# A linear attention layer on one core: values and gates as seven half products over two pairs of heads

## The chip, the cores and the metric

The kernel runs on 1 core of a Trainium2 chip. The metric is the time of one execution in device microseconds (us), of which the median of some runs is taken. TensorE (PE) multiplies matrices, VectorE (DVE), ScalarE (ACT) and GpSimd (POOL) work elementwise, SyncE (SP) issues transfers. DRAM is the device's memory; SBUF and PSUM are on the core, and PE writes only PSUM.

## What is computed

The program is two blocks of a network over 2048 tokens of 512 features: a recurrent unit, a state space layer, feed forward layers, an attention, two mixtures of experts. The change touches one layer, the linear attention (`L1_attn_b`), which takes the normalized residual x:

```
qkv = silu(x @ qkv_w.T)                    # 32 heads of 64, each with q, k, v
per head and block i of tokens:
    intra = ((q_i @ k_i.T) * decay) @ v_i
    inter = (q_i * query_decay) @ state
    state = state * block_decay + (k_i * key_decay).T @ v_i
attn = rmsnorm(intra + inter over all heads) * norm_w
y    = (sigmoid(x @ gate_w.T) * attn) @ out_w.T
```

## The kernel before

Every layer is a stage of its own: it has a program for each engine, and all engines meet at its end. The linear attention consists of three stages. `lina` (`normalized_features`, L131) normalizes the residual `g.X` and transposes it to `lin_z`, features by tokens. `linb` (`linear_heads`, L2241) is the part that the change is about. `linc` is the output projection.

`linb` works through 16 pairs of heads n. Each pair is 128 features wide and has four quarters q of 512 tokens, each of four chunks of 128. For a quarter PE does `keys_first` (the scores `s_ps`, and `tr_ps`, the transposed keys), `additions` (`kv_ps`, what the keys and values add to the state) and `outputs` (`o_ps`, from the values and from the state). DVE multiplies queries by decays (`qd`) and scores by decays (`aw`), updates the state (`update`) and makes the `gated` result, which SP stores. ACT copies `tr_ps` with a decay (`kt`) and `o_ps` to `osb`. POOL squares `osb` (`linb_sq`) and adds it up in `lin_squares`.

Among this, PE computes the next pair's features, in three banks of PSUM, `pr_ps`. `piece` (L2409) makes the values in the first quarter (kind 2: tokens as the stationary operand, matmuls of 128 columns) and the gates in the second (kind 3: weights as the stationary operand, 512 columns), over all of the 512 features, and ACT takes each out of its bank through silu or sigmoid. In the third and fourth quarters `seven` (L2437) makes queries and keys together, for half of the tokens each: a product of 2 x 2 blocks (two weight blocks by two halves of the features, against two halves of the features by two quarters of the tokens) as seven products of half the depth in place of eight. These need sums of the weights, which POOL makes (`weight_sums`, L2378, four a pair), sums of the tokens' features, which DVE makes once (`token_sums`, L2630, eight, stored where the residual was), and then, on the way out, a copy `p1` on ACT and five sums u2, u3, kB, kA, qB on DVE, with silu on ACT behind them. PE issues the products in the order p1, p6, p2, p7, p5, p4, p3; p7 waits for u2, p4 for u3, p3 for kB. The first two stand ahead of `additions`, the others behind it. Queries, keys and gates lie in `proj`, values in `vt`, both for two pairs in turn.

The order on each engine is that of the code, and semaphores hold the engines together. The stage begins with POOL's constants (decay tables, 64 small memsets for the slopes); PE waits for all of them (L2521), and ACT then computes the decays, 32 single columns of `kdec` among them. SP loads pair 0's weights, copies the residual to DRAM (`normalized_rows`, since the token sums overwrite it), and clears `residual_rows`, 4 MB, with `linb_nothing` once the constants are there. It fetches the residual back at the last pair.

## Time and profile before

| | us |
|---|---|
| median of 3 runs | 5027.12 (5025.49 to 5028.86) |
| the profiled execution | 5025.78 |
| its span | 5024.1 |
| stage `linb` in it, from the first instruction to the last square | 2934.6 to 4095.6 |
| PE busy in the span | 4532.5 |

All times of the trace are microseconds from the span's start. A line number is the code line before the change; a matmul with f32 operands stands in the trace as two instructions.

### The profile page before, as it was taken

The numbers are of one execution on the slowest core, as the hardware profiler recorded it, in microseconds if no ns is written. First come the engines' busy times: TensorE is split into PE (matmuls) and PEld (weight loads), VectorE is DVE, ScalarE is ACT, GpSimd is POOL, SyncE is SP. The second block draws the span as 40 slices with busy tenths as digits, with TensorE's granted clock in tenths as the row PEclk, the third lists the DMA queues.
The fourth block names the chain that finished last, engine by engine and source line by source line (L and its number), as shares of the span: only waits on it lengthen the run. The fifth ranks groups of instructions, "written<-read, shape, count | busy, mean of one in ns | idle before, by whom it ended". The sixth has DMA issues, their size and how long they took to land. (4 is left out here: it accounts for less than half of the span.)

```text
span 5024.1 us, 65280 instructions
## 1 busy us (share of the span) xinstructions
PE 4532.5 (90%) x26052; PEld 2544.3 (51%) x26052; DVE 2503.2 (50%) x3810; ACT 1646.6 (33%) x2825; POOL 1704.5 (34%) x1130
## 2 busy tenths in 40 slices
PE   6359997899999999978999859999999989699996
PEld 3124443433333333245666536666666658566663
DVE  7865888367777777852222234444443444512222
ACT  5414443211555556822111123323333210321110
POOL 2000000101888887024555411222222210155553
PEclk9679998999999999988999979999999999799998
DMA  2000000100000000036888740000010033378897
GB/s 75 0 16 7 7 0 31 40 1 1 2 1 2 1 1 1 1 129 182 257 257 258 168 157 24 32 32 32 25 33 32 24 132 105 134 223 257 257 257 198
DMA packets 241716, 425.99 MB, mean 85 GB/s; under 512 B 31504, under 2 KB 119568, under 8 KB 241424
## 3 DMA queue, kind: packets, MB, share of 16 engines
q1 hardware_dynamic: 184080, 279.28, 16.7%
q0 software_dynamic: 57344, 142.64, 11.6%
q8 instruction: 205, 3.36, 0.3%
q14 instruction: 87, 0.71, 0.0%
HBM read 301.73 MB, written 120.13 MB: 84 GB/s over the span
## 5 line engine op out<-in xcount | busy, mean ns | idle before, releaser
L1557 ACT ACTIVATE attc_prob<-attc_ps 128x512 f32<-128x512 f32 x1024 | 547.6, 597 | 299.0 <-PE attc_ps L1473 289.8
L1589 DVE TENSOR_REDUCE attc_peak<-attc_ps 128x1 f32<-128x512 f32 x768 | 490.7, 682 | 204.6 <-PE attc_ps L1481 204.6
L1444 POOL TENSOR_TENSOR attc_acc<-attc_acc,attc_prob 128x2048 f32<-128x2048 f32 x120 | 543.3, 4528 | 40.4 <-ACT attc_prob L1557 26.5
L1481 PE MATMUL attc_ps<-att_k,att_q 32*128 32x512 f32 x1536 | 492.0, 641 | 0.0
L1473 PE MATMUL attc_ps<-att_q,att_k 32*128 32x512 f32 x2048 | 459.7, 589 | 0.0
L2398 POOL TENSOR_TENSOR linb_sq<-linb_osb 128x512 f32<-128x512 f32 x64 | 90.8, 1419 | 847.3 <-ACT linb_osb L2588 847.3
L1493 PE MATMUL attc_ps<-attc_prob,att_v 128*32 128x256 f32 (+1 forms) x3472 | 310.4, 429 | 0.4 <-ACT attc_prob L1557 0.4
L1074 DVE TENSOR_TENSOR_SCAN ssmb_state<-ssmb_decay,ssmb_bu 128x2048 f32<-128x2048 f32 x64 | 280.7, 4413 | 54.2 <-PE ssmb_y_ps L927 29.4
L2072 POOL DMA_INDIRECT residual_rows<-moe2c_ye,moe2w_index x128 | 201.7, 1575 | 230.1 <-DVE moe2c_ye L2195 200.2
L2072 POOL DMA_INDIRECT residual_rows<-moe1c_ye,moe1w_index x128 | 201.5, 1575 | 230.0 <-DVE moe1c_ye L2195 200.0
L2698 DVE SCALAR_TENSOR_TENSOR linb_gated<-linb_osb,linb_norm_w,linb_proj 128x512 f32<-128x512 f32 x64 | 61.3, 957 | 400.4 <-ACT linb_osb L2588 400.4
L927 PE MATMUL ssmb_y_ps<-ssmb_state,ssmb_diag 128*128 128x512 f32 x512 | 234.9, 606 | 19.5 <-DVE ssmb_y L1083 9.9
L2424 PE MATMUL linb_pr_ps<-linb_wt,lin_z 128*128 128x128 f32 x2048 | 236.3, 277 | 17.0 <-POOL linb_slope_own L2375 17.0
L783 POOL MEMSET ffn_nothing<- 128x512 f32 x2 | 1.0, 524 | 716.6 <-POOLq L61 716.6
L2424 PEld LDWEIGHTS linb_pr_ps<-linb_wt,lin_z 128*128 128x128 f32 x2048 | 233.5, 194 | 17.2 <-POOL linb_slope_own L2375 17.2
L1493 PEld LDWEIGHTS attc_ps<-attc_prob,att_v 128*32 128x32 f32 x3472 | 68.4, 108 | 329.5 <-ACT attc_prob L1557 180.2
L2105 PE MATMUL moe2c_gu_ps<-moe2c_xt,moe2w_wgu 128*128 128x256 f32 x1024 | 232.5, 381 | 0.0
L2105 PE MATMUL moe1c_gu_ps<-moe1c_xt,moe1w_wgu 128*128 128x256 f32 x1024 | 232.4, 380 | 0.0
L2428 PE MATMUL linb_pr_ps<-lin_z,linb_wt 128*128 128x512 f32 x512 | 224.9, 592 | 0.0
L2187 DVE TENSOR_TENSOR moe1c_h<-moe1c_sg,moe1c_gu_ps 128x256 f32<-128x256 f32 x96 | 40.4, 421 | 326.3 <-ACT moe1c_sg L2169 309.3
L2187 DVE TENSOR_TENSOR moe2c_h<-moe2c_sg,moe2c_gu_ps 128x256 f32<-128x256 f32 x96 | 40.4, 421 | 326.2 <-ACT moe2c_sg L2169 309.3
L2105 PEld LDWEIGHTS moe2c_gu_ps<-moe2c_xt,moe2w_wgu 128*128 128x128 f32 x1024 | 190.6, 191 | 23.5
(488 smaller groups left out, 8545.8 us busy)
## 6 DMA issues: line engine op xcount, KB each, us to landing
moe1w_wgu<-in_L_ffn_gate_up_proj SPq DMA_DIRECT2D x32, 1536.0 KB
moe2w_wgu<-in_L_ffn_gate_up_proj SPq DMA_DIRECT2D x32, 1536.0 KB
moe1w_wd<-in_L_ffn_down_proj SPq DMA_DIRECT2D x32, 512.0 KB
gated_features<-linb_gated SPq DMA_DIRECT2D x64, 256.0 KB, 2.3
moe2w_wd<-in_L_ffn_down_proj SPq DMA_DIRECT2D x32, 512.0 KB
linc_gt<-gated_features SPq DMA_DIRECT2D x7, 2048.0 KB, 8.6
linb_wt<-in_L_attn_b_qkv_w SPq DMA_DIRECT2D x16, 768.0 KB, 4.8
residual_rows<-residual SPq DMA_DIRECT2D x8, 1024.0 KB, 4.3
```

The lines of the kernel that those rows point to most:

```text
L927: last = nc.tensor.matmul(y_ps[:, t, :], diag[:, s % DIAGS, :], state[:, s % RING, t * NB:(t + 1) * NB], start=(n == 0), stop=(n == N_STAT ...
L1074: V.tensor_tensor_scan(state[:, s % RING, :], decay[:, s % RING, :], bu[:, e % 2, :], 0.0, ALU.mult, ALU.add).then_inc(state_done, 1)
L1444: pool.tensor_tensor(to, before, prob[:, U % NP, :, :], ALU.add).then_inc(pool_done, 2 if at % HALF == 1 else 1)
L1473: nc.tensor.matmul(ps[:, bank_of(("score", U, h)), :], k[own, f, keys], q[own, f, cols], start=False, stop=True).then_inc(s_done, 1)
L1481: nc.tensor.matmul(ps[:, take("peak", U, h), :], q[own, f, i * P:(i + 1) * P], k[own, f, b * NB:(b + 1) * NB], start=True, stop=True).then ...
L1493: last = nc.tensor.matmul(o_bank[h * DH:(h + 1) * DH, cols], v[:, i, at:at + DH], prob[:, U % NP, h, cols], start=(i == 0), stop=(i == TT ...
L1557: nc.scalar.activation(prob[:, U % NP, h, :], ps[:, bank_of(("score", U, h)), :], ACT.Exp).then_inc(exp_done, 1)
L1589: V.tensor_reduce(peak[:, w // TT % 2, i % QH, h, b:b + 1], ps[:, bank_of(("peak", U, h)), :], axis=AX.X, op=ALU.max).then_inc(mx_used, 1)
L2072: pool.indirect_dma_start(out=g.y_dram[x], out_offset=bass.IndirectOffsetOnAxis(ap=index[:, n // 2, n % 2:n % 2 + 1], axis=0), in_=ye[:, y ...
L2105: last = nc.tensor.matmul(gu_ps[:, x, part, :], wgu[:, j % PW, x, k, part * IN:part * IN + P], xt[:, j % 2, x, k, :], start=(k == 0), stop ...
L2424: last = nc.tensor.matmul(bank[:, c * CH:(c + 1) * CH], z[:, k, (t * TQ + c) * CH:(t * TQ + c + 1) * CH], wt[:, b, kind, k, :], start=(k = ...
L2428: last = nc.tensor.matmul(bank, wt[:, b, kind, k, :], z[:, k, tokens(t)], start=(k == 0), stop=(k == DT - 1))
```

## The change

Values and gates are now also made by `seven`, over two pairs of heads m at once (the two weight blocks are then the two pairs) and half of the tokens. So each pair n computes ahead one seven of values, one of gates and two of queries and keys: in an even pair values and gates of the late half of the tokens for this pair and the next, in an odd pair those of the early half for the next two. A table `sevens` sets the order. Values and gates keep early and late halves in buffers of their own; queries and keys lie in one buffer, `qk`, for one pair, and ACT waits for `qd` before it writes there. Each kind has its own weight sums (`wsum` is three times as large), POOL makes those of values and gates once in two pairs, and the weights of values and gates lie in a buffer `wvg` outside the stage. Its first contents and the copy of the residual to DRAM are loaded and stored in the norm stage (`moves`). At the start, four sevens come without a wait for the constants; POOL makes three groups of weight sums ahead of the constants; the decays come between two results of the third seven, with `kdec` in one instruction. (The code that `seven_out` and `sums` share with before is the same but for the place of the result.)

```diff
-def normalized_features(nc, g, name, zt, weights=()):
...
-            if weights:
-                sp.wait_ge(w_loaded, 16 * len(weights))
+            for to, source in moves:
+                sp.dma_start(to, source).then_inc(w_loaded, 16)
+            if weights or moves:
+                sp.wait_ge(w_loaded, 16 * (len(weights) + len(moves)))
...
+def value_weights(g, m):
+    return g.dram["L1_attn_b_qkv_w"][2 * m:2 * m + 2, :, 2, :, :].rearrange("n p k f -> p n k f")
+
+
+def gate_weights(g, m):
+    return g.dram["L1_attn_b_gate_w"][2 * m:2 * m + 2, :, :, :].rearrange("n p k f -> p n k f")
...
+        with nc.sbuf_tensor("lin_z", [P, DT, T], F32) as z, nc.sbuf_tensor("lin_wvg", [P, 2, 2, DT, P], F32) as wvg:
+            x_rows = g.z_dram[0:T, 0:D].rearrange("(i p) d -> p i d", p=P)
+            normalized_features(nc, g, "lina", z, moves=((wvg[:, 0, :, :, :], value_weights(g, 0)), (wvg[:, 1, :, :, :], gate_weights(g, 0)),
+                                                         (x_rows, g.X[:, :, :])))
+            linear_heads(nc, g, "linb", z, wvg, x_rows, squares)
...
-        wt = L.sb("wt", [P, 2, KINDS, DT, P])
-        proj = [L.sb(f"proj{b}", [P, 3, T]) for b in range(2)]
...
+        first = [(VALUES, 0, 0), (GATES, 0, 0), (QK, 0, 0), (QK, 0, 1)]
+
+        def sevens_of(n):
+            if n + 1 == PAIRS_L:
+                return []
+            early = [(VALUES, n // 2, 1), (GATES, n // 2, 1)] if n % 2 == 0 else [(VALUES, n // 2 + 1, 0), (GATES, n // 2 + 1, 0)]
+            return early + [(QK, n + 1, 0), (QK, n + 1, 1)]
+
+        sevens = first + [s for n in range(PAIRS_L) for s in sevens_of(n)]
+        place = {what: i for i, what in enumerate(sevens)}
+        wqk = L.sb("wqk", [P, 2, 2, DT, P])
+        qk = L.sb("qk", [P, 2, T])
+        g_early, g_late = L.sb("g_early", [P, 3, 2, NB]), L.sb("g_late", [P, 2, 2, NB])
+        v_early, v_late = L.sb("v_early", [P, 3, HC, P]), L.sb("v_late", [P, 2, HC, P])
...
+        def needed_by(n, q):
+            return (QK, n, q // 2) if q < 2 or n % 2 or n + 1 == PAIRS_L else (GATES, n // 2, 1)
...
+        def weights(kind, m):
+            return wqk[:, m % 2, :, :, :] if kind == QK else wvg[:, kind, :, :, :]
+
+        def values(n, c):
+            return v_early[:, n % 3, c, :] if c < HC else v_late[:, n % 2, c - HC, :]
+
+        def gates(n, q):
+            return g_early[:, n % 3, q, :] if q < 2 else g_late[:, n % 2, q - 2, :]
+
+        def result(kind, m, half, t):
+            if kind == QK:
+                return qk[:, half, tokens(t)]
+            if kind == GATES:
+                return gates(2 * m + half, t)
+            rows = v_early[:, (2 * m + half) % 3, :, :] if t < 2 else v_late[:, half, :, :]
+            return rows[:, t % 2 * TQ:(t % 2 + 1) * TQ, :].rearrange("p c f -> p (c f)")
...
+            def load(n):
+                sp.dma_start(wqk[:, n % 2, :, :, :], qkv_rows[n, :, 0:2, :, :]).then_inc(w_loaded[n % 2], 16)
+
+            load(0)
+            load(1)
...
             for n in range(PAIRS_L):
                 if n + 2 < PAIRS_L:
-                    reload(n, n % 2)
+                    sp.wait_ge(pr_done, after_seven((QK, n, 1)))
+                    load(n + 2)
...
+                    sp.wait_ge(gated_done, n * TC + (q + 1))
+                    sp.dma_start(out_rows[:, n, tokens(q)], gated[:, q % 2, :]).then_inc(saved[q % 2], 16)
+                    if n % 2 == 0 and n + 2 < PAIRS_L and q == 0:
+                        sp.wait_ge(pr_done, after_seven((VALUES, n // 2, 1)))
+                        sp.dma_start(wvg[:, VALUES, :, :, :], value_weights(g, n // 2 + 1)).then_inc(v_loaded, 16)
+                    if n % 2 == 0 and n + 2 < PAIRS_L and q == 1:
+                        sp.wait_ge(pr_done, after_seven((GATES, n // 2, 1)))
+                        sp.dma_start(wvg[:, GATES, :, :, :], gate_weights(g, n // 2 + 1)).then_inc(g_loaded, 16)
...
+                if kind == QK:
+                    pool.wait_ge(w_loaded[m % 2], 16 * (m // 2 + 1))
+                elif m:
+                    pool.wait_ge(v_loaded if kind == VALUES else g_loaded, 16 * m)
+                if m:
+                    pool.wait_ge(pr_done, after_seven((kind, m - 1, 1)))
...
+            weight_sums(VALUES, 0)
+            weight_sums(GATES, 0)
+            weight_sums(QK, 0)
...
-            link(pool.memset(state[:, :, :], 0.0))
-            link(pool.memset(squares[:, :], 0.0))
-            link(pool.memset(nothing[:, :], 0.0))
             for h, s in enumerate(head_slopes()):
                 link(pool.memset(slope_all[:, h:h + 1], -s))
                 r = (h % 2) * LD
                 link(pool.memset(slope_own[r:r + LD, h // 2:h // 2 + 1], -s))
+            link(pool.tensor_tensor(until[:, :], until[:, :], slope_all[:, :], ALU.mult))
+            link(pool.memset(state[:, :, :], 0.0))
+            link(pool.memset(squares[:, :], 0.0))
+            link(pool.memset(nothing[:, :], 0.0))
             assert link.n == N_CONSTS
...
+            for n in range(PAIRS_L):
+                if n + 1 < PAIRS_L:
+                    weight_sums(QK, n + 1)
                 for q in range(TC):
+                    if q == 2 and n % 2 == 0 and n + 2 < PAIRS_L:
+                        weight_sums(VALUES, n // 2 + 1)
+                        weight_sums(GATES, n // 2 + 1)
                     m = n * TC + q
-                    pool.wait_ge(o_out, m + 3)
+                    pool.wait_ge(o_out, m + 1)
                     pool.tensor_tensor(sq[:, :], osb[:, q % 2, :], osb[:, q % 2, :], ALU.mult).then_inc(sq_step, 1)
...
+            def product(kind, bank, w, x, fresh):
+                for c in range(TQ if kind == VALUES else 1):
+                    chunk = slice(c * CH, (c + 1) * CH)
+                    for k in range(HK):
+                        if kind == VALUES:
+                            last = nc.tensor.matmul(pr_ps[:, bank, chunk], x[:, k, chunk], w[:, k, :],
+                                                    start=(fresh and c == 0 and k == 0), stop=(k == HK - 1), skip_group_check=True)
+                        else:
+                            last = nc.tensor.matmul(pr_ps[:, bank, :], w[:, k, :], x[:, k, :],
+                                                    start=(fresh and k == 0), stop=(k == HK - 1), skip_group_check=not fresh)
                 last.then_inc(pr_done, 1)
...
                 if "p1" in some:
-                    pe.wait_ge(pr_out, n * FROM_BANKS + (2 * TC + 2 if x else 2 * TC - 1))
-                    product(one, a11, b11, True)
+                    if kind == QK:
+                        pe.wait_ge(w_loaded[m % 2], 16 * (m // 2 + 1))
+                    elif m:
+                        pe.wait_ge(v_loaded if kind == VALUES else g_loaded, 16 * m)
+                    if i:
+                        pe.wait_ge(pr_out, 2 * i)
+                    product(kind, one, a11, b11, True)
                 if "p6" in some:
...
+                if q % 2 == 0:
+                    pe.wait_ge(pr_out, copies_of(needed_by(n, q)))
+                    pe.wait_ge(finished, finished_of(needed_by(n, q)))
+                if m:
+                    pe.wait_ge(aw_done, m)
...
-            pe.sem_inc(kv_done, 1)
-            pe.wait_ge(consts, N_CONSTS)
-            for kind in (2, 3):
-                for t in range(TC):
-                    piece(kind, t, 0, 0, 0)
-            for x in range(2):
-                seven(0, 0, x, PRODUCTS)
...
+            for what in first:
+                seven(what, PRODUCTS)
+            for n in range(PAIRS_L):
+                more = sevens_of(n)
                 for q in range(TC):
-                    keys_first(n, b, q)
-                    if more and q < 2:
-                        piece(q + 2, 0, n + 1, r + b, 1 - b)
-                    elif more:
-                        seven(n + 1, 1 - b, q - 2, PRODUCTS[0:2])
-                    additions(n, b, q)
-                    if more and q < 2:
-                        for t in range(1, TC):
-                            piece(q + 2, t, n + 1, r + b, 1 - b)
-                    elif more:
-                        seven(n + 1, 1 - b, q - 2, PRODUCTS[2:])
-                    outputs(n, b, q)
-
-            over_pairs(body)
+                    keys_first(n, q)
+                    if more:
+                        seven(more[q], PRODUCTS[0:2])
+                    additions(n, q)
+                    if more:
+                        seven(more[q], PRODUCTS[2:])
+                    outputs(n, q)
...
+            def decays():
+                act.wait_ge(consts, N_CONSTS)
+                nc.scalar.activation(sdec[:, :], slope_own[:, :], ACT.Exp, scale=float(CH)).then_inc(tables0, 1)
+                nc.scalar.activation(kdec[:, :], until[:, :], ACT.Exp).then_inc(tables0, 1)
+                table(0)
...
+                nc.scalar.activation(result(kind, m, 0, 2 * x), pr_ps[:, 0, :], shape).then_inc(pr_out, 1)
+                if what == (QK, 0, 0):
+                    decays()
+                for name, half, t in (("kB", 1, 2 * x + 1), ("kA", 1, 2 * x), ("qB", 0, 2 * x + 1)):
+                    act.wait_ge(added, after_sum(i, name))
+                    to = result(kind, m, half, t)
+                    nc.scalar.activation(to, to, shape).then_inc(finished, 1)
...
-                        for t in range(TC):
-                            piece_out(q + 2, t, n + 1, 1 - b)
+                        act.wait_ge(qd_done, n * TC + q + 1)
+                        seven_out(more[q])
                         if q == 1:
-                            table(n + 1, 1 - b)
-                    elif more:
-                        seven_out(n + 1, 1 - b, q - 2)
+                            table(n + 1)
                     quarter_out(n, q)
...
+            for x in range(2):
+                token_sums(x)
+            for what in first:
+                sums(what, SUMS)
+            dve.wait_ge(tables0, 2)
+            dve.wait_ge(norm_loaded, 16)
+            for n in range(PAIRS_L):
+                more = sevens_of(n)
                 dve.wait_ge(tables, n * 3 + 3)
...
+                    if q % 2 == 0:
+                        dve.wait_ge(pr_out, copies_of(needed_by(n, q)))
+                        dve.wait_ge(finished, finished_of(needed_by(n, q)))
+                    if m:
+                        dve.wait_ge(o_done, m)
+                    V.tensor_tensor(qd[:, :].rearrange("p (c i) -> p c i", i=CH), qk[:, 0, tokens(q)].rearrange("p (c i) -> p c i", i=CH),
...
-                    if more and q >= 2:
-                        sums(n + 1, 1 - b, q - 2, ("u2",))
+                                    dd[:, n % 2, :, :].rearrange("p h (o i) -> p h o i", o=1).to_broadcast([P, 2, TQ, CH]), ALU.mult).then_inc(aw_done, 1)
+                    if more:
+                        sums(more[q], ("u2",))
                     update(n, q)
...
+                    if more:
+                        sums(more[q], SUMS[1:])
+                    dve.wait_ge(o_out, m + 1)
+                    if m >= 2:
...
-            dve.wait_ge(x_spilled, 16)
-            for x in range(2):
-                token_sums(x)
-            for x in range(2):
-                sums(0, 0, x, SUMS)
-            over_pairs(body)
```

How this stands on the engines. The counts here are those of the program, half of the trace's for matmuls. PE, from the start of `linb` (the names are output<-operands), before:

```order
L2424 MATMUL linb_pr_ps<-linb_wt,lin_z 128x128 x64
L2428 MATMUL linb_pr_ps<-lin_z,linb_wt 128x512 x16
L2433 MATMUL linb_pr_ps<-lin_z,linb_wt 128x512 x2
L2433 MATMUL linb_pr_ps<-residual,linb_wsum 128x512 x2
L2433 MATMUL linb_pr_ps<-lin_z,linb_wt 128x512 x2
```

and with the change (one whole seven of values, then the one of gates begins):

```order
L2459 MATMUL linb_pr_ps<-lin_wvg,lin_z 128x128 x8
L2459 MATMUL linb_pr_ps<-linb_wsum,residual 128x128 x8
L2459 MATMUL linb_pr_ps<-lin_wvg,lin_z 128x128 x8
L2459 MATMUL linb_pr_ps<-linb_wsum,residual 128x128 x16
L2459 MATMUL linb_pr_ps<-lin_wvg,residual 128x128 x8
L2459 MATMUL linb_pr_ps<-linb_wsum,lin_z 128x128 x8
L2462 MATMUL linb_pr_ps<-lin_z,lin_wvg 128x512 x2
```

64 small matmuls of values are now 56, and those of gates, 16, are 14. The second product and those behind it have sums as operands.

PE, first quarter of the first pair, from the scores to the outputs, before:

```order
L2482 MATMUL linb_s_ps<-linb_proj 128x128 x8
L2488 MATMUL linb_tr_ps<-ident,linb_proj 128x128 x4
L2424 MATMUL linb_pr_ps<-linb_wt,lin_z 128x128 x16
L2497 MATMUL linb_kv_ps<-linb_vt,linb_kt 128x128 x4
L2424 MATMUL linb_pr_ps<-linb_wt,lin_z 128x128 x48
L2509 MATMUL linb_o_ps<-linb_aw,linb_vt 64x128 x8
```

and with the change:

```order
L2517 MATMUL linb_s_ps<-linb_qk 128x128 x8
L2524 MATMUL linb_tr_ps<-ident,linb_qk 128x128 x4
L2459 MATMUL linb_pr_ps<-lin_wvg,lin_z 128x128 x8
L2459 MATMUL linb_pr_ps<-linb_wsum,residual 128x128 x8
L2533 MATMUL linb_kv_ps<-linb_v_early,linb_kt 128x128 x4
L2459 MATMUL linb_pr_ps<-lin_wvg,lin_z 128x128 x8
L2459 MATMUL linb_pr_ps<-linb_wsum,residual 128x128 x16
L2459 MATMUL linb_pr_ps<-lin_wvg,residual 128x128 x8
L2459 MATMUL linb_pr_ps<-linb_wsum,lin_z 128x128 x8
L2545 MATMUL linb_o_ps<-linb_aw,linb_v_early 64x128 x8
```

The four pieces of values became seven products, two of them ahead of `linb_kv_ps` as in the other quarters.

SP, from the start of the norm stage `lina` (whose first row is the first branch), before:

```order
L140 UNCONDITIONAL_BRANCH
L2313 UNCONDITIONAL_BRANCH
L2316 DMA linb_wt<-in_L_attn_b_qkv_w 128x1536
L2317 DMA linb_wt<-in_L_attn_b_gate_w 128x512
L2335 DMA normalized_rows<-residual 128x16x512
```

and with the change:

```order
L140 UNCONDITIONAL_BRANCH
L145 DMA lin_wvg<-in_L_attn_b_qkv_w 128x2x512
L145 DMA lin_wvg<-in_L_attn_b_gate_w 128x2x512
L145 DMA normalized_rows<-residual 128x16x512
L58 UNCONDITIONAL_BRANCH
L2359 UNCONDITIONAL_BRANCH
L2362 DMA linb_wqk<-in_L_attn_b_qkv_w 128x1024 x2
```

The residual's copy and 1 MB of weights moved from `linb` into `lina`, and the weights of queries and keys alone stayed.

## Rows read from the trace of the kernel before

**Rows 1.** Page, part 1: busy us, share of the span, instructions.

```profile
PE 4532.5 (90%) x26052; PEld 2544.3 (51%) x26052; DVE 2503.2 (50%) x3810; ACT 1646.6 (33%) x2825; POOL 1704.5 (34%) x1130
```

**Rows 2.** Busy time by stretches: start:end, length, engines, clock, DMA share, GB/s.

```profile
core 0: us, PE busy (x) PEld busy (x) DVE busy (x) ACT busy (x) POOL busy (x), PEclk, DMA share, GB/s
3080.00:4010.00 930.00, 930.00 (x5604) 622.21 (x5603) 380.61 (x685) 279.72 (x472) 197.41 (x161) 1.00 0.09 30
```

**Rows 3.** In order of time, PE, POOL, DVE: start, length, engine, line, what, [idle before].

```profile
3570.79 3.74 PE L2424 MATMUL linb_pr_ps<-linb_wt,lin_z 128*128 128x128 f32 x32
...
3574.36 1.06 PE L2497 MATMUL linb_kv_ps<-linb_vt,linb_kt 128*128 128x128 f32 x8
...
3571.65 1.60 POOL L2400 TENSOR_TENSOR lin_squares<-lin_squares,linb_sq 128x512 f32<-128x512 f32 x1
...
3572.05 1.21 DVE L2689 TENSOR_TENSOR linb_aw<-linb_s_ps,linb_dd 128x1024 f32<-128x1024 f32 x1
```

**Rows 4.** In order of time, PE, start and end of the layer.

```profile
2950.11 16.95 PE L2424 MATMUL linb_pr_ps<-linb_wt,lin_z 128*128 128x128 f32 x128 [16.97 <-POOL linb_slope_own L2375]
...
2980.63 1.88 PE L2433 MATMUL linb_pr_ps<-lin_z,linb_wt 128*128 128x512 f32 x4
...
2992.65 1.88 PE L2433 MATMUL linb_pr_ps<-lin_z,linb_wt 128*128 128x512 f32 x4
...
3006.32 1.16 PE L2482 MATMUL linb_s_ps<-linb_proj 64*128 64x128 f32 x16 [1.49 <-issue]
...
4061.72 1.16 PE L2482 MATMUL linb_s_ps<-linb_proj 64*128 64x128 f32 x16
```

**Rows 5.** In order of time, POOL and DVE, the sums at the start.

```profile
2950.24 0.73 POOL L2385 TENSOR_TENSOR linb_wsum<-linb_wt 128x256 f32<-128x256 f32 x1 [0.19 <-POOL linb_slope_own L2375]
...
2956.27 1.23 DVE L2634 TENSOR_TENSOR residual<-lin_z 128x1024 f32<-128x1024 f32 x1 [23.91 <-ACT linb_kdec L2595]
...
2964.46 1.23 DVE L2639 TENSOR_TENSOR residual<-lin_z,residual 128x1024 f32<-128x1024 f32 x1
```

**Rows 6.** In order of time, ACT, POOL, DVE, from second to third quarter.

```profile
3604.37 0.60 ACT L2560 ACTIVATE linb_proj<-linb_pr_ps 128x512 f32<-128x512 f32 x1 [2.84 <-PE linb_pr_ps L2428]
...
3607.88 1.54 POOL L2398 TENSOR_TENSOR linb_sq<-linb_osb 128x512 f32<-128x512 f32 x1 [16.44 <-ACT linb_osb L2588]
3609.50 1.60 POOL L2400 TENSOR_TENSOR lin_squares<-lin_squares,linb_sq 128x512 f32<-128x512 f32 x1
...
3608.67 1.30 DVE L2686 TENSOR_TENSOR linb_qd<-linb_proj,linb_qdec 128x512 f32<-128x512 f32 x1
...
3611.60 0.69 DVE L2647 TENSOR_TENSOR linb_u<-linb_pr_ps,linb_p 128x512 f32<-128x512 f32 x1 [0.37 <-PE linb_pr_ps L2433]
```

**Rows 7.** In order of time, PE and ACT, end of a seven.

```profile
3619.16 1.88 PE L2433 MATMUL linb_pr_ps<-lin_z,linb_wsum 128*128 128x512 f32 x4
...
3623.08 1.16 PE L2482 MATMUL linb_s_ps<-linb_proj 64*128 64x128 f32 x16
...
3621.80 0.63 ACT L2571 ACTIVATE linb_proj<-linb_proj 128x512 f32<-128x512 f32 x1 [1.09 <-DVE linb_proj L2657]
```

**Rows 8.** In order of time, SyncE and ACT; transfers: count, KB each, us to landing.

```profile
2934.58 0.35 SPq L2316 DMA_DIRECT2D linb_wt<-in_L_attn_b_qkv_w  x1
...
2935.45 0.43 SPq L2335 DMA_DIRECT2D normalized_rows<-residual  x1
...
2916.77 1.28 ACT L128 ACT_TABLE_LOAD   x1 [56.00 <-PEq L61]
...
2932.81 1.07 ACT L184 COPY lin_z<-lina_zt_ps 128x512 f32 x2 [0.54 <-PE lina_zt_ps L169]
...
normalized_rows<-residual SPq DMA_DIRECT2D x1, 4096.0 KB, 15.6
```

**Rows 9.** Busy time by stretches: first products, last pair.

```profile
2950.00:2952.00 2.00, 1.89 (x9) 1.89 (x10) 0.00 (x0) 1.91 (x11) 1.81 (x4) 0.50 1.02 414
...
4074.00:4076.00 2.00, 0.66 (x11) 0.45 (x8) 1.48 (x6) 0.00 (x0) 0.00 (x0) 1.00 1.05 389
```

326 lines of the change are left out of this document (121 added, 205 removed).

## The prediction

> **What bounds the kernel now.** I read the page's line on TensorE (PE) first, then the stretches of the layer, then one pair in order of time, then the layer's first 75 us engine by engine, then the transfers. Over the whole program PE is busy 90% of the time [rows 1]. Inside this layer, from 3080 to 4010 us, it is busy 930.00 of 930.00 us at a granted clock of 1.00, while DVE, ACT and POOL are busy 41%, 30% and 21% of it [rows 2]. So here only PE's own work counts, and time taken off it is gained as long as no other engine becomes late. From the first scores at 3006.32 to those of the last pair at 4061.72 [rows 4] it is 1055.40 us, 15 periods of 70.36 us, one for each pair that computes the next one's features ahead. The one place where PE waits long is the start: the first product comes at 2950.11, after 16.97 us of idleness that POOL's constants end [rows 4].
>
> **The loop (removed PE work).** A values matmul of 128 columns costs 0.1116 us of PE: 32 of them from 3570.79 to 3574.36 [rows 3]. One of 512 columns costs 0.4293 us: the 28 of one seven take 2980.63 to 2992.65, 12.02 us [rows 4]. (The trace shows each matmul of the program twice.) Before, a pair costs 128 of the first and 32 of the second for values and gates: 14.28 + 13.74 = 28.02 us. After, it costs one values seven, 7 products of 16 small ones, 112 x 0.1116 = 12.50 us, and one gates seven, 28 x 0.4293 = 12.02 us: 24.52 us. The gain is 3.50 us per pair, for 15 pairs: **-52.5 us**, a period of 66.86 us. Both kinds are issued back to back in the trace before, so I take no other price for them.
>
> **The loop (added work).** Each of these sevens adds five sums on DVE at 0.69 us and one more pass of 0.6 us on ACT, about 7 us of DVE per pair; with 41% busy it has room. What counts is whether PE waits in the middle. The nearest rows are the sevens of queries and keys, which already run with no wait of PE, beside the largest batch of state updates. Three differences remain.
> (1) After the gates seven, the last result goes through DVE and ACT, which in a seven ends 1.55 us behind PE's last product (3619.16 + 1.72 = 3620.88, ACT done at 3621.80 + 0.63) [rows 7]; before, ACT's pass over the last gates product began 0.2 us behind it, at 3604.37, and took 0.60, 0.8 in all [rows 6]. So tables, output copy, gated result and aw come 0.75 us later in the next quarter. There u2 would start at 3611.60 + 0.75 and end at 3613.04, and the product behind it starts at 3614.00 (3619.16 less three products of 1.72) [rows 6, 7]: 1.0 us to spare. Cost 0.
> (2) In even pairs the scores of the third quarter now wait for that gates seven. They start 2.20 us behind its last product, as the scores at 3623.08 do behind 3620.88 [rows 7], and its result is there after 1.55: 0.65 us to spare. In return no pair's first scores wait for the seven just ahead. Cost 0.
> (3) ACT now waits for qd ahead of each seven; behind that wait stand the copy of p1 and the finishing passes, and for the copy wait u2 and PE's third product. In the third quarter qd ends at 3608.67 + 1.30 = 3609.97, with (1) at 3610.72, and the copy ends at 3611.3; PE's third product starts at 3612.28. Cost 0.
> From the other side: should all three bite, I bound them by 1 us a pair, 15 us.
>
> **POOL and DVE.** POOL gets eight more weight sums per two pairs, 0.73 us each [rows 5], 5.8 us, in the third quarter of even pairs, behind the square and the sum that end at 3609.50 + 1.60 = 3611.10 [rows 6]; the next square comes a quarter, some 16 us, later. Do they hold up DVE? In the trace they collide where both operands lie in SBUF: qd takes 1.30 us and u2, of the same size but out of PSUM, 0.69 [rows 6]. POOL's square ends at 3607.88 + 1.54 = 3609.42, and qd, started at 3608.67, ends 0.55 behind that; they take turns. The new sums fall beside DVE's sums out of PSUM, and such an instruction isn't held: aw, 1024 columns out of PSUM, takes 1.21 us wholly beside POOL's sum of 3571.65 to 3573.25 [rows 3], as long as a token sum of 1024 columns alone, 1.22 [rows 5]. Cost 0.
> The Trainium skill ("SBUF — State Buffer", "Who interferes with whom") states the same as a rule: a DVE instruction with two SBUF inputs and a GpSimd instruction that reads SBUF exclude each other for the whole instruction, with at most one SBUF input DVE is free. By its letter every token sum at the start would wait for one weight sum, 8 x 1.90 = 15.2 us, and the start would gain 11.7 us.
>
> **The start.** PE no longer waits for the constants. The stage's first instructions stand at 2934.6 [rows 8]. p1 of values runs at once. p6 needs four token sums (DVE) and four weight sums (POOL), and p7 needs u2, which stands behind all eight token sums. These last 9.42 us alone (2956.27 to 2964.46 + 1.23), 1.17 each [rows 5]; if they take turns with POOL's at 0.73, 1.90 each, 15.2 us. I take 14.0, nearer to turns, because of the qd row. u2 ends at 2934.6 + 14.0 + 0.8 = 2949.4. Then four products of values, 7.14, and three sevens, 36.06: 2992.6. Before, the first 128 matmuls took from 2950.11 to 2966.89 (2980.63 less 32 of 0.4293), 16.8 us rather than 14.3 [rows 4], since the clock first stood at 0.50 [rows 9]; now p6 and p2 run in that time, so I add 0.8 (bounds 0 and 2.5): 2993.4. The first scores follow at once, for they wait only for the first half of queries and keys. Before they stand at 3006.32 [rows 4]: **-12.9 us**. Bounds: -18.3 (no turns, no cold clock) and -10.0 (full turns, full loss). ACT needs the constants only in the third seven, near 2974; POOL, with twelve sums (to 2951.5) and 15.6 us of constants (2934.6 to 2950.2) [rows 5, 8], has them at 2967: 7 us to spare. The 4 MB of clearing transfers start there too and, at the 15.6 us that 4 MB take [rows 8], end before the loop's first load at 2993.
>
> **The norm stage (moved transfers).** The 4 MB copy of the residual and 1 MB of weights now start with the norm stage, at 2916.77 [rows 8] less some 0.1, and its end waits for them. Before, the first issue was at 2934.58, and the copy, issued at 2935.45 behind the same 1 MB, landed 15.6 us later, at 2951.05: 16.5 us in all [rows 8]. That gives 2933.2, and ACT's last copy there ends at 2933.88 [rows 8]. **Hidden, by 0.7 us**; cost 0. If the new weight loads, in runs of 2 KB, went at half rate, 2.6 us more, and the start would be 2 us later.
>
> The tail (last pair, the way back of the residual) is the same work behind the same product. **Sum**: -52.5 - 12.9 = -65.4 us against the profiled execution's 5025.8 (its span of 5024.1 and 1.7 around it), 4960.4; the median of 5027.1 lies 1.3 above that, so 4961.7 us.
>
> **Rivals.**
> A. *As above*, 4961.7, each term within its bounds. For it: PE without any wait in 930 us, and sevens already in that run.
> B. *New waits inside the loop.* The margins of 0.65 and 1.0 us are eaten (DVE behind POOL in the third quarter, the finishing pass late); 30 new sevens at 0.5 us cost 15: 4976.7.
> C. *No turns at the start.* Token sums at 1.17 us each: u2 at 2944.8, scores at 2988.8, -17.5 instead of -12.9: 4957.1. Against it: the qd row.
> D. *The residual's copy ends the norm stage.* It lands 4 us later than reckoned: 4965.7. For it: only 0.7 us to spare.
> E. *The change doesn't give what it says*: a small matmul in a seven would not keep 0.1116 us but cost 0.128 (14.28 over 112); the values seven is then as dear as the plain one, +1.8 x 16: 4990. Against it: in size and kind the instructions are the same.
> F. *Slower than before: the clock.* If PE's waits in the new sevens got long enough to pull the granted clock to 0.50 (the 1.2 GHz level), each us of work costs two. It decides once 65.4 us of the loop's work, 4.4 us of each pair's 66.9, run at that level beyond what waits cost; with a quarter of each pair so, 16.7 us x 15 = 250 us: 5212. Against it: in the last pair PE is busy 0.66 of 2.00 us in a stretch and its clock stays at 1.00 [rows 9]; it fell only over the 17 us of full idleness ahead of 2950.
>
> **How the numbers follow.** A 0.68, B 0.13, C 0.09, D 0.04, E 0.03, F 0.03. The time is that of A. The range goes from 4953 (C, less what median and profile differ by and 3 us) to 4976 (D whole, B nearly): it leaves out F, E and the end of B, and the unforeseen. A measurement of this kernel can tell about 0.2%, 10 us, from no change; A to E are all faster by more: faster 0.96, same 0.01, slower 0.03.
>
> **What would show it.** In the profile of the changed kernel: a period of 66.9 us from pair to pair, PE busy throughout at clock 1.00; the first scores about 58.8 us after the layer's first instruction (71.7 before); token sums with 1.7 to 1.9 us between starts; ACT's first exponentials without a wait for POOL; the norm stage no longer than 18 us. Wrong it would be with a PE wait ahead of p7, p4 or the third quarter's scores, or a norm stage that ends with a wait of SyncE.

## The result, and the profile after

The changed kernel takes 4963.79 us (median of 4 runs, 4961.65 to 4964.71) beside 5027.61 us for the kernel before on the same chip: a ratio of 0.9873, with a 95% interval of 0.9857 to 0.9888. It is 63.8 us faster. The forecast was 4961.7 us, a gain of 65.4.

The page's first part of the changed kernel, which answers to [rows 1], and then its busy time in the loop (start:end, length, then the engines, the granted clock, the share of the DMA engines, GB/s), which answers to [rows 2]:

```profile
PE 4478.5 (90%) x25730; PEld 2509.3 (51%) x25732; DVE 2621.7 (53%) x3970; ACT 1663.2 (34%) x2827; POOL 1754.6 (35%) x1195
```

```profile
3080.00:3940.00 860.00, 860.00 (x5117) 566.61 (x5116) 465.08 (x802) 290.48 (x488) 222.78 (x203) 1.00 0.10 31
```

PE still has no idle time at all in the loop, at a clock of 1.00. DVE went from 41% to 54% of it (465.08 of 860.00), and that costs nothing.

PE in order of time in the changed kernel, as in [rows 4] (start, length, engine, line, what, [idle before, what ended it]): the first products of the layer, its first scores, and those of the last pair.

```profile
2935.79 3.48 PE L2459 MATMUL linb_pr_ps<-lin_wvg,lin_z 128*128 128x128 f32 x16 [1.45 <-PEq L61]
2942.76 3.61 PE L2459 MATMUL linb_pr_ps<-linb_wsum,residual 128*128 128x128 f32 x16 [3.50 <-DVE residual L2645]
2946.17 2.03 PE L2459 MATMUL linb_pr_ps<-lin_wvg,lin_z 128*128 128x128 f32 x16
2949.98 3.84 PE L2459 MATMUL linb_pr_ps<-linb_wsum,residual 128*128 128x128 f32 x32 [1.78 <-DVE linb_u L2655]
...
2957.23 1.88 PE L2462 MATMUL linb_pr_ps<-lin_z,lin_wvg 128*128 128x512 f32 x4
...
2993.38 1.16 PE L2517 MATMUL linb_s_ps<-linb_qk 64*128 64x128 f32 x16
...
3996.27 1.16 PE L2517 MATMUL linb_s_ps<-linb_qk 64*128 64x128 f32 x16
```

From the first scores to those of the last pair it is 1002.89 us, 15 periods of 66.86 (before 1055.40, 70.36). The stage `linb` starts with SyncE's load at 2935.75, so the first scores stand 57.6 us into it (before 71.7). The 16.97 us for which PE waited for POOL's constants are gone. What is left are 3.50 us until four token sums are there (the second product, p6) and 1.78 until u2 is (the fourth, p7).

The norm stage, SyncE and ACT in order of time, and the issue's row (KB, us to landing), as in [rows 8]:

```profile
2918.76 0.46 SPq L145 DMA_DIRECT2D normalized_rows<-residual  x1
...
2935.75 0.82 SPq L2362 DMA_DIRECT2D linb_wqk<-in_L_attn_b_qkv_w  x2
...
2917.83 1.28 ACT L128 ACT_TABLE_LOAD   x1 [55.68 <-PEq L61]
...
2933.91 1.13 ACT L186 COPY lin_z<-lina_zt_ps 128x512 f32 x2 [0.48 <-PE lina_zt_ps L171]
```

```profile
normalized_rows<-residual SPq DMA_DIRECT2D x1, 4096.0 KB, 15.5
```

The copy lands at 2918.76 + 15.5 = 2934.3, ACT ends at 2933.91 + 1.13 = 2935.04: the copy is hidden, and the stage takes 17.9 us (2917.83 to 2935.75) where it took 17.8.

**Where the 63.8 us are.** The loop gives 52.5 and the start 14.1, together 66.6. The last pair and the way to the next stage `linc` take 35.25 us (3996.27 to 4031.52) where they took 35.47. The profiled executions differ by 64.3 us in their spans, so 2.3 are lost elsewhere, in code that the change doesn't touch: 1.1 ahead of the norm stage and 1.8 where the last layer goes from routing to experts (over six microseconds at the experts' first large products the granted clock was 0.80 before, 4400 to 4406 us, and 0.59 now, 4334 to 4340), and 0.6 won in between. Over the fourteen profiles of this study the norm stage starts anywhere from 2916.77 to 2920.67, with the same code ahead of it. That spread is as large as some effects below, so these are read inside the stage: **scores** is the distance from the start of `linb` (SyncE's first load) to its first scores, **tail** from the last pair's first scores to PE's first matmul of `linc`.

| kernel | median us | norm stage | scores | period | tail |
|---|---|---|---|---|---|
| before | 5027.6 to 5028.3 | 17.8 | 71.7 | 70.36 | 35.5 |
| changed | 4963.8 | 17.9 | 57.6 | 66.86 | 35.3 |
| changed, again | 4964.4 | 17.7 | 57.6 | 66.86 | 37.9 |
| eighth | 5019.0 | 17.9 | 61.1 | 70.36 | 35.3 |
| spill_back | 4975.5 | 17.8 | 68.7 | 66.86 | 36.7 |
| consts_first | 4971.9 | 17.9 | 70.1 | 66.86 | 35.3 |
| pool_yields | 4960.1 | 18.1 | 55.6 | 66.86 | 36.2 |
| norm_5mb | 4962.5 | 19.6 | 57.6 | 66.86 | 35.3 |
| pad2 | 4964.0 | 17.8 | 57.6 | 66.86 | 35.3 |
| pad4 | 4991.0 | 18.0 | 57.6 | 67.9, then 68.93 | 35.3 |
| pad6 | 5083.8 | 17.7 | 57.6 | 71.4, then 73.8 to 75.6 | 36.4 |
| pool_double | 4963.9 | 18.0 | 57.6 | 66.86 | 35.3 |
| late_token_sums | 4960.2 | 17.8 | 55.5 | 66.86 | 35.3 |
| early_p2 | 4959.3 | 17.7 | 53.2 | 66.86 | 36.4 |

Medians are of 4 runs (eighth 10, pool_double one; before 4 to 13). The last four columns are from one profiled execution of each kernel. Where a median and these columns differ by some microseconds (consts_first is 8.2 above the changed kernel in the median and 11.8 in the profiled execution), the difference is no larger than the spread just named.

### The profile page after: what moved, and what is told of

It reads as the page before. It is cut to its first block and busy times, and to the rows that moved or that the text cites. A ratio compares the mean times of both kernels' runs of the same rounds, so it can differ in the third digit from the quotient of the medians.

```text
span 4959.8 us, 64998 instructions
## 1 busy us (share of the span) xinstructions
PE 4478.5 (90%) x25730; PEld 2509.3 (51%) x25732; DVE 2621.7 (53%) x3970; ACT 1663.2 (34%) x2827; POOL 1754.6 (35%) x1195
## 3 DMA queue, kind: packets, MB, share of 16 engines
q0 software_dynamic: 57344, 142.64, 11.8%
## 5 line engine op out<-in xcount | busy, mean ns | idle before, releaser
L2462 PE MATMUL linb_pr_ps<-residual,linb_wsum 128*128 128x512 f32 x576 | 262.9, 593 | 0.0
L2107 PEld LDWEIGHTS moe1c_gu_ps<-moe1c_xt,moe1w_wgu 128*128 128x128 f32 x1024 | 190.9, 191 | 23.0
L1306 DVE TENSOR_REDUCE attb_peak<-attb_mx_ps 128x2 f32<-128x1024 f32 x128 | 150.9, 1221 | 94.1 <-PE attb_mx_ps L1245 93.9
L2462 PEld LDWEIGHTS linb_pr_ps<-residual,linb_wsum 128*128 128x128 f32 x576 | 109.7, 190 | 137.5 <-issue 137.5
```

The lines of the kernel that those rows point to most:

```text
L1306: V.tensor_reduce(peak[:, tb % 2, i % QH, 2 * hp:2 * hp + 2, b], mx_ps[:, 2 * hp:2 * hp + 2, :], axis=AX.X, op=ALU.max).then_inc(mx_used, 1)
L2107: last = nc.tensor.matmul(gu_ps[:, x, part, :], wgu[:, j % PW, x, k, part * IN:part * IN + P], xt[:, j % 2, x, k, :], start=(k == 0), stop ...
L2462: last = nc.tensor.matmul(pr_ps[:, bank, :], w[:, k, :], x[:, k, :], start=(fresh and k == 0), stop=(k == HK - 1), skip_group_check=not fresh)
```

## The experiments

My theory: the loop is PE's passes and nothing else; the start is the removed wait, less token sums that take turns with POOL; the moved copy is hidden by less than a microsecond. The rivals are those of the prediction: waits inside the loop, no turns, the copy as the norm stage's end, and a falling clock.

**1. The passes given back**

```
-            def product(kind, bank, w, x, fresh):
+            def product(kind, bank, w, x, fresh, eighth=False):
+                if eighth:
+                    product_once(kind, bank, w, x, fresh)
+                product_once(kind, bank, w, x, fresh).then_inc(pr_done, 1)
...
-                    product(kind, three, s4, b22, False)
+                    product(kind, three, s4, b22, False, eighth=kind != QK)
```

(`product_once` is the old `product` without its count, so the count of finished products is raised once for both. The kernel computes other values and gates than the layer asks for; its work on the other engines is the same.)

> The changed kernel with an eighth product in each seven of values and gates: the last product (p3) is issued twice, so that its term is added twice; nothing else moves. This gives PE back exactly the passes that the change removed. My theory (PE's passes are the whole of the loop's gain, nothing waits): 15 pairs x (1.79 + 1.72) = 52.6 us and 3.5 us more at the start, so 4963.8 + 56.1 = 5019.9 us, period 70.4 us, PE busy throughout. Rival (the sevens hide waits that the passes filled, or other engines' work sets the period): less than 45 us more, period under 69.8.

Measured: 5018.99 us, +55.2 on the changed kernel's 4963.8; between the starts of `linb` and `linc` +56.0. The period is 70.36 us, to the hundredth that of the kernel before. In the trace of this kernel, PE in order of time, the doubled products are:

```profile
3573.00 3.74 PE L2464 MATMUL linb_pr_ps<-linb_wsum,lin_z 128*128 128x128 f32 x32
...
3591.33 3.60 PE L2467 MATMUL linb_pr_ps<-lin_z,linb_wsum 128*128 128x512 f32 x8
```

So 52.5 us of the loop's gain are the removed products, one for one. Had the sevens brought a wait of PE of their own, this kernel would have been slower than 70.36 a pair.

**2. The copy back in its old place**

```
+            dve.wait_ge(x_spilled, 16)
             for x in range(2):
                 token_sums(x)
```

(and the copy issued in `linb` behind the first load.)

> The changed kernel with the residual's 4 MB copy issued in linb again, behind the first weight load, and DVE's token sums waiting for it. Theory: it is issued at 0.5 us into linb and lands 15.6 us later, 16.1 us after the stage's first instruction; the eight token sums then run alone at 1.17 us and u2 ends at 16.1 + 9.4 + 0.7 = 26.2 instead of 14.2: the first scores come 12.0 us later (at 69.6 instead of 57.6), 4975.8 us. Rival (the copy was also hidden here, by the constants or by POOL): 0 to 3 us.

Measured: 4975.51 us, +11.7. Scores at 68.7 instead of 57.6, +11.0; 1.4 more are in the tail (below). DVE in this kernel:

```profile
2951.34 1.23 DVE L2642 TENSOR_TENSOR residual<-lin_z 128x1024 f32<-128x1024 f32 x1 [16.82 <-DMA normalized_rows<-residual]
...
2960.73 0.68 DVE L2657 TENSOR_TENSOR linb_u<-linb_pr_ps,linb_p 128x512 f32<-128x512 f32 x1
```

The first token sum is released by the transfer. The size is 1.0 less than the 12.0 expected: the copy landed 14.2 us after its issue, not 15.6, with half a megabyte ahead of it instead of one; in return p6 (3.75 us) and p2 (2.47) ran in part at the 1.2 GHz level (mean granted clock 0.60 from 2956.2 to 2962) and ended 0.7 us behind u2. Of the start's 14.1 us, then, 11.0 hang on the moved copy: without it the constants' wait would have been exchanged for the copy's. The rival (hidden anyway) falls.

**3. The constants first again**

```
+            pe.wait_ge(consts, N_CONSTS)
             for what in first:
                 seven(what, PRODUCTS)
```

(and POOL's twelve weight sums behind its constants.)

> The changed kernel with the old order at the start of linb: POOL makes its constants first and PE waits for them, then POOL's weight sums. Theory: PE's first product comes 15.6 us into the stage, the cold clock costs 2.5, and the four sevens (12.5 + 36.1) follow without a wait: first scores at 66.7 instead of 57.6, 9.1 us later, 4972.9 us. Token sums, now beside POOL's constants and no weight sums, take 1.17 us each instead of 1.69. Rival (token sums slow for another reason, such as the weight transfers): still 1.69.

Measured: 4971.94 us, +8.2; in the profiled execution, which is 11.8 longer than the changed kernel's, scores at 70.1, +12.5. The direction is the theory's, the size is not: PE's first product comes at 18.7 us, not at 15.6. The eight token sums start 1.20 us apart (the first at 2935.88, the last at 2944.26), so the rival, which kept them at 1.69, falls. POOL and DVE in order of time in this kernel, with POOL's same cast in the changed kernel as the last row:

```profile
2935.85 0.23 POOL L2417 IOTA linb_dist_i<- 128x128 int32 x1 [52.46 <-POOLq L61]
2936.15 1.09 POOL L2418 CAST linb_dist<-linb_dist_i 128x128 f32<-128x128 int32 x1
2937.41 1.07 POOL L2419 TENSOR_SCALAR_AFFINE_SELECT linb_dist<-linb_dist 128x128 f32<-128x128 f32 x1 [0.16 <-POOL linb_dist L2418]
...
2937.02 1.31 DVE L2642 TENSOR_TENSOR residual<-lin_z 128x1024 f32<-128x1024 f32 x1
```

```profile
2952.36 0.29 POOL L2421 CAST linb_dist<-linb_dist_i 128x128 f32<-128x128 int32 x1
```

Four constants that read SBUF (two casts and the select of 128 columns, one cast of 32) take 3.90 us together beside DVE's token sums, where alone they take 0.29, 0.29, 0.29 and 0.21; that is 2.8 of the 3.1 us (0.3 is the constant that the change adds, the product for the decays). IOTA and the memsets, which read nothing, keep their 0.23 and 0.10. The token sums lose 0.1. So the turns are not between sums only, and the short instruction pays most. The Trainium skill ("SBUF — State Buffer", "Who interferes with whom") names any GpSimd instruction that reads SBUF; by that rule, the trace agrees, and my expectation should have had it.

**4. POOL steps aside**

```
             weight_sums(VALUES, 0)
+            pool.wait_ge(z_summed, 8)
             weight_sums(GATES, 0)
```

> The changed kernel with POOL waiting for all eight token sums behind the weight sums of values, so that the last four token sums have no weight sums beside them. Theory (a token sum and a weight sum take turns because both read two operands in SBUF): the first four keep 1.69 us between starts, the last four take 1.17 us; u2 ends 2 us earlier, PE's fourth product follows the third at once, 1.8 us earlier, and the scores stand at 55.8 instead of 57.6: 4962.0. Rival (they are slow for another reason: weight transfers, the first instructions of a stage): all eight at 1.69, no change.

Measured: 4960.10 us, -3.7; scores at 55.6, -2.1 (55.8 expected). DVE in this kernel, the first and the fifth token sum and u2; then POOL, its second weight sum beside them and its fifth alone:

```profile
2936.54 1.80 DVE L2641 TENSOR_TENSOR residual<-lin_z 128x1024 f32<-128x1024 f32 x1 [2.23 <-PEq L61]
...
2943.26 1.21 DVE L2641 TENSOR_TENSOR residual<-lin_z 128x1024 f32<-128x1024 f32 x1
...
2947.92 0.68 DVE L2656 TENSOR_TENSOR linb_u<-linb_pr_ps,linb_p 128x512 f32<-128x512 f32 x1
```

```profile
2937.21 1.71 POOL L2410 TENSOR_TENSOR linb_wsum<-lin_wvg 128x256 f32<-128x256 f32 x1
...
2948.08 0.74 POOL L2409 TENSOR_TENSOR linb_wsum<-lin_wvg 128x256 f32<-128x256 f32 x1 [5.83 <-DVE residual L2646]
```

The four sums beside POOL's take 6.72 us from start to start, the four without them 4.66. In the changed kernel the last four, in the same place but beside POOL's sums, take 6.71 (2942.54 to 2949.25), and no transfer runs there, since those of the stage's start have landed by 2941.6. So the turns are shown to be the cause, and rival C of the prediction falls.

**5. One more megabyte in the norm stage**

```
-                                                         (x_rows, g.X[:, :, :])))
+                                                         (x_rows, g.X[:, :, :]),
+                                                         (g.g_dram[0:P, 0:4 * D].rearrange("p (i d) -> p i d", i=4), g.X[:, 0:4, :])))
```

> The changed kernel with 1 MB more copied in the norm stage, behind the residual's copy (rows 0 to 511 of the residual into a scratch that is overwritten later). The residual's copy lands 0.8 us before ACT's last copy ends there. Theory (the copy is hidden by 0.8 us only): a quarter of 15.5 us is 3.9, so the stage ends 3.1 us later, 21.0 instead of 17.9 us, 4966.9. Rival (the two run at different rates, or the copy already ended the stage): 3.9 or more; or under 1.

Measured: the stage takes 19.6 us, +1.7, which is neither the theory's +3.1 nor the rival's 3.9 or under 1; the whole, 4962.52, shows nothing of it (within the spread named above). The issues' rows of this kernel:

```profile
normalized_rows<-residual SPq DMA_DIRECT2D x1, 4096.0 KB, 15.4
gated_features<-residual SPq DMA_DIRECT2D x1, 1024.0 KB, 17.3
```

The second is issued 0.5 us behind the first and lands 2.4 later, not 3.9. The 15.5 us of the copy are not all its own: 1 MB of weights runs ahead of it, and in the changed kernel the transfers reach 400 to 414 GB/s only from the fifth microsecond behind its issue on; at that rate 4 MB take 10.2 us and one more megabyte 2.6. The sign is as expected (what lands later than ACT's end lengthens the stage), the price of a megabyte there was too high by more than a half.

**6. Dummy work ahead of u2**

```
+                    if more and q < 2:
+                        for _ in range(2):
+                            dve.wait_ge(padded, len(pads))
+                            pads.append(V.tensor_tensor(pad[:, :], z[:, 0, 0:NB], z[:, 1, 0:NB], ALU.add).then_inc(padded, 1))
                     if more:
                         sums(more[q], ("u2",))
```

(This is pad2; pad4 has 4 and pad6 has 6 in place of the 2. `padded` only keeps the dummy sums in order.)

> As pad6, but with two dummy sums ahead of u2 in the first and second quarter. They take 1.4 us in the second quarter, where 1.74 are spare, and 1.4 to 2.1 in the first, where 1.81 and 1.3 of idle time are. Theory (the margins are what the trace shows): no change, period 66.86 us, at most 0.3 us per seven. Rival (the chain through u2 already sets the pace in places, so that the kernel stands on the edge): 0.5 us or more per seven, 15 us or more.

> The changed kernel with six dummy sums of 512 columns on DVE (two inputs in SBUF, 0.7 us each alone) ahead of u2 in the first and second quarter of each pair, so in the new sevens. u2 ends 1.81 and 1.74 us before PE needs it. In the second quarter they take 4.2 us, 2.4 more than there is; in the first they also take turns with four weight sums of POOL and take about 7.2, 1.3 of it in idle time, 4.1 more than there is. Theory: PE waits 6.5 us per pair, 15 pairs: +98 us (range 75 to 110), 5062, and the granted clock stays at 1.00. Rival F of the prediction (such waits pull the clock to 0.50): at least 4.4 us of each pair at half speed beyond the waits, +65 us or more on top, and 0.50 in the stretches behind the waits.

> As pad6, with four dummy sums. In pad6 PE waited 2.60 us in each values seven and 2.25 in each gates seven, and behind nearly every such wait the granted clock stood at 0.50 for 3.4 us, which cost another 1.75: 120 us in all. With two sums less, u2 ends 1.4 to 1.9 us earlier, so PE waits 0.8 in each of the 30 new sevens. Theory 1 (short waits cost only themselves; in other stretches PE waits 0.4 to 0.9 us with the clock at 1.00): +25 us (15 to 40), 4989. Theory 2 (every wait in the loop makes the clock fall behind it): 30 x (0.8 + 1.75), +77, 5041.

Measured: pad2 4964.00 us and a period of 66.86: the margins read from the trace are there. pad6 5083.77 us, +120 where 98 (75 to 110) were expected. pad4, made after that, 4991.03, +27 (25 expected by theory 1, 77 by theory 2), a period of 68.93. In pad6 PE waits 2.25 us in each gates seven (2.4 reckoned) but only 2.60 in each values seven (4.1 reckoned: the six sums there took 5.96 us beside POOL's weight sums, not 7.2); what goes beyond the waits is the clock. PE in pad6, a values and two gates sevens; then in pad4:

```profile
3527.11 5.46 PE L2460 MATMUL linb_pr_ps<-linb_wsum,residual 128*128 128x128 f32 x32 [2.59 <-DVE linb_u L2656]
...
3548.02 5.40 PE L2463 MATMUL linb_pr_ps<-residual,linb_wsum 128*128 128x512 f32 x8 [2.26 <-DVE linb_u L2656]
...
3173.77 3.70 PE L2463 MATMUL linb_pr_ps<-residual,linb_wsum 128*128 128x512 f32 x8 [2.25 <-DVE linb_u L2656]
```

```profile
3553.44 3.84 PE L2460 MATMUL linb_pr_ps<-linb_wsum,residual 128*128 128x128 f32 x32 [0.74 <-DVE linb_u L2656]
```

And the stretches of pad6 behind the first and the third of them (clock: the column ahead of the last two):

```profile
3528.00:3531.00 3.00, 3.00 (x18) 3.00 (x17) 1.88 (x6) 0.00 (x0) 0.00 (x0) 0.55 0.00 0
...
3173.00:3176.00 3.00, 2.23 (x5) 1.06 (x6) 2.76 (x10) 0.00 (x0) 0.00 (x0) 1.00 0.00 0
```

p7 and p5 together take 3.74 us in a values seven and 3.60 in a gates seven at full clock, and 5.46 and 5.40 behind a wait: PE was at 2.4 GHz and wholly busy up to the wait, idle for 2.3 to 2.6 us, and then stood at 1.2 GHz for most of these two products. In 25 of the 29 waits of pad6 it fell so; in four it did not (every fourth pair, in the gates seven, where the period is 73.80 instead of 75.56). That is 25 x 1.75 = 44 us of the 120. Why these four were spared isn't shown. Waits of 0.74 and 0.81 us, 29 of them in pad4, left the clock at 1.00 throughout, so theory 1 holds and theory 2 falls. So rival F was half right: its mechanism exists in this loop, at waits of 2.3 us though not of 0.8, each such wait costs 1.7 to 1.8 times itself, and pad6 is slower than the kernel before (5083.8 against 5028.3 us). The changed kernel is far from it, with no wait at all.

The prediction held against F that the clock had fallen only over 17 us of full idleness. That was a misreading of the kernel before, where it fell much sooner. PE's last work in the norm stage, and the two stretches behind it:

```profile
2932.03 1.10 PE L169 MATMUL lina_zt_ps<-ident,lina_z 128*128 128x128 f32 x8 [0.51 <-DVE lina_z L152]
```

```profile
2933.00:2935.00 2.00, 0.14 (x2) 0.00 (x0) 0.00 (x0) 1.15 (x3) 0.33 (x2) 0.92 0.00 0
2935.00:2937.00 2.00, 0.00 (x0) 0.00 (x0) 0.00 (x0) 1.01 (x1) 1.51 (x7) 0.50 0.76 132
```

PE ended at 2933.13, and before 2935 the clock was at the 1.2 GHz level.

**7. POOL's added work doubled**

```
                     if q == 2 and n % 2 == 0 and n + 2 < PAIRS_L:
+                        for _ in range(8):
+                            pool.wait_ge(padded, len(pads))
+                            pads.append(pool.tensor_tensor(pad[:, :], z[:, 0, 0:HK * P], z[:, 1, 0:HK * P], ALU.add).then_inc(padded, 1))
                         weight_sums(VALUES, n // 2 + 1)
```

> The changed kernel with eight dummy sums on POOL (128x256, two inputs in SBUF, 0.73 us) ahead of the weight sums of values and gates in the third quarter of every second pair, so twice the added POOL work. Theory: they stand beside DVE sums that read PSUM and are over before POOL's next square, 16 us behind the last: no change, period 66.86 us, DVE's sums there still 0.69 us. Rival (B of the prediction, POOL holds up DVE in the third quarter): DVE's sums or state updates longer there and some tenths of a us more in every second pair.

Measured: 4963.90 us (one run), period 66.86. POOL's dummies, and one of DVE's sums beside the weight sums behind them:

```profile
3570.05 6.39 POOL L2447 TENSOR_TENSOR linb_pad<-lin_z 128x256 f32<-128x256 f32 x8
...
3577.48 0.69 DVE L2668 TENSOR_TENSOR linb_qk<-linb_pr_ps,linb_p 128x512 f32<-128x512 f32 x1 [0.96 <-PE linb_pr_ps L2467]
```

One detail was just missed: POOL's last weight sum ended at 3582.22 and held its next square back by 0.2 us. Nobody waited for it.

**8. Two versions, and the changed kernel beside them**

```
-            for x in range(2):
-                token_sums(x)
-            for what in first:
+            token_sums(0, (0, 1))
+            for i, what in enumerate(first):
+                if i in (1, 2):
+                    token_sums(1, (i - 1,))
                 sums(what, SUMS)
```

(`token_sums(x, parts)` makes the first two of the four sums of half x for part 0, the last two for part 1), and for early_p2 also

```
+        FIRST = ("p1", "p2", "p6", "p7", "p5", "p4", "p3")
...
-            for what in first:
+            for p in FIRST:
+                seven(first[0], (p,))
+            for what in first[1:]:
                 seven(what, PRODUCTS)
```

> The changed kernel itself, as the yardstick beside the two versions: 4963.8 us, within 0.05%.

> The changed kernel with the second four token sums taken out from ahead of u2: two stand ahead of the gates seven's u2 and two ahead of the next seven's, in idle times of 2.74 us; only the fourth seven reads them. Theory: u2 waits for the sixth product only and PE's 1.78 us of waiting there goes: first scores at 55.8 instead of 57.6 us from the stage's start, 4962.0. Rival (the moved sums hold up u2 of the gates seven): 0 to 1 us back.

> As late_token_sums, and in the very first seven PE issues p2 ahead of p6: p2 needs only ACT's copy of p1, p6 needs four token sums. Theory: p2 falls into the 3.50 us in which PE waits for the token sums; the product that stood behind p6 (2.0 us) is gone from the path, but u2 now follows p6 at once and PE waits about 0.7 us for it: 1.0 to 1.5 us more than late_token_sums, the first scores near 54.5, 4960.7. Rival (the clock stays at 0.50 for the same number of columns, so p6 is as slow as before and nothing is won): as late_token_sums.

Measured: 4964.36, 4960.24 and 4959.32 us, scores at 57.6, 55.5 and 53.2. PE in early_p2: p2, p6 and p7; then the stretch of its p6, and that of p6 in the changed kernel (clock: the column ahead of the last two):

```profile
2942.70 2.05 PE L2460 MATMUL linb_pr_ps<-lin_wvg,lin_z 128*128 128x128 f32 x16 [0.68 <-ACT linb_p L2592]
2945.41 2.02 PE L2460 MATMUL linb_pr_ps<-linb_wsum,residual 128*128 128x128 f32 x16 [0.65 <-DVE residual L2650]
2948.21 3.84 PE L2460 MATMUL linb_pr_ps<-linb_wsum,residual 128*128 128x128 f32 x32 [0.78 <-DVE linb_u L2660]
```

```profile
2945.40:2947.40 2.00, 2.00 (x16) 1.83 (x16) 0.00 (x0) 0.00 (x0) 1.92 (x4) 1.00 0.04 8
```

```profile
2942.80:2946.20 3.40, 3.40 (x17) 3.40 (x18) 3.40 (x3) 0.00 (x0) 3.40 (x3) 0.52 0.02 5
```

late_token_sums gives 2.1 us, a little more than the wait of 1.78. early_p2 gives 2.3 more, not 1.0 to 1.5: p6 takes 2.02 us where it took 3.61, at a clock of 1.00 where it was 0.52: ahead of it PE had worked on p2 and waited only 0.68 and 0.65 us, in the changed kernel it had waited 3.50. The rival (clock still down) falls for p6. Inside the stage both beat the changed kernel by more than the scores vary (57.6 in all seven profiles in which the start is as in the changed kernel); in the whole time early_p2's 5 us are about the spread of single runs (4956.55 to 4964.87 beside 4961.91 to 4966.84). Against the kernel before early_p2 is at 0.9859 (0.9843 to 0.9876). pool_yields gets the first 2.1 us with one line.

## Why the prediction was right, point by point

**The loop, -52.5.** Exact: 66.86 us a pair. Experiment 1 shows that it is the products and that nothing was given back. Rival E (small matmuls dearer in a seven) would have left 1.8 us more in the period, 68.66, and falls.

**The three margins.** All three hold, as the changed kernel's rows of the third quarter of an even pair show (DVE, PE, ACT; to be read with [rows 6] and [rows 7]):

```profile
3567.34 0.67 DVE L2655 TENSOR_TENSOR linb_u<-linb_pr_ps,linb_p 128x512 f32<-128x512 f32 x1
...
3569.56 3.60 PE L2462 MATMUL linb_pr_ps<-residual,linb_wsum 128*128 128x512 f32 x8
...
3561.92 1.16 PE L2517 MATMUL linb_s_ps<-linb_qk 64*128 64x128 f32 x16
...
3560.64 0.63 ACT L2597 ACTIVATE linb_g_late<-linb_g_late 128x512 f32<-128x512 f32 x1 [1.09 <-DVE linb_g_late L2665]
...
3566.31 0.58 ACT L2589 COPY linb_p<-linb_pr_ps 128x512 f32<-128x512 f32 x1 [1.53 <-DVE linb_qd L2702]
```

u2 ends at 3568.01, 1.55 us ahead of p7 (1.0 forecast: the 0.75 were added to a start of u2 that had 0.37 us of idleness ahead of it, [rows 6], and these took up part of them); the gates' last result is there at 3561.27, 0.65 ahead of the scores (0.65 forecast); the copy of p1 ends at 3566.89, 0.95 ahead of PE's third product at 3567.84. Rival B falls by this and by pad2.

**POOL's added sums, 0.** Right, with twice as many too (experiment 7).

**The start, -12.9.** It gave -14.1. The step that was mis-sized is the sum to the first scores. The token sums took 13.5 us, not 14.0: they start 1.68 apart, less than the 1.90 of full turns. And the 0.8 us that I added for the cold clock did not arise: p1 and p6 do run slowly (3.48 and 3.61 us, by their rows), but the time lies inside the wait for the sums, which ends later anyway. It comes to the surface once the sums are early (experiment 8). The turns themselves, the larger choice of the two, are shown by experiment 4. By the Trainium skill's rule read to the letter ("SBUF — State Buffer", "Who interferes with whom"), 15.2 us for the eight, an estimate with the durations of [rows 5], it would have been a gain of 11.7; the trace agrees on who takes turns, but each turn is about 0.2 us shorter than the sum of the two durations. That this gain exists only together with the moved copy (11.0 of the 14.1, experiment 2) the prediction had only implied: it costed the copy at nothing in its new place, and never priced the old place.

**The norm stage, 0.** Right: 17.9 us, with the copy landing 0.8 us ahead of ACT's end (forecast 0.7). Rival D falls. The reserve is real and small, as experiment 5 shows; but the rate behind it, 15.6 us for 4 MB, mixed the copy with what ran ahead of it.

**The tail, 0.** Right for the profiled execution, but my evidence for it was thin. The last pair of the changed kernel in two executions of the same code, 4010 to 4014 us:

```profile
4010.00:4014.00 4.00, 2.81 (x28) 2.36 (x28) 1.77 (x3) 1.35 (x3) 1.64 (x2) 1.00 0.75 283
```

```profile
4010.00:4014.00 4.00, 2.66 (x19) 2.44 (x20) 1.40 (x5) 0.59 (x1) 0.22 (x1) 0.73 0.92 337
```

In the second the mean clock is 0.73 there and 0.51 from 4022 to 4026 us, and the tail takes 37.9 us instead of 35.3. It fell in five of the fourteen profiles, that of the kernel before not among them, and costs 0.9 to 2.6 us each time. I had read one stretch of [rows 9] with a clock of 1.00 as a rule.

**The sum.** 65.4 forecast, 66.6 inside the layer, 63.8 in the medians. The difference between the last two is code ahead of and behind the layer that didn't change. That the total came within 2.1 us of the forecast is therefore in part luck: the layer gave 1.2 us more than forecast, and about 2.3 were lost outside it, for which the sum has no term. A term of 1 or 2 us can't be seen in the whole time of this kernel.
